# Where the Gelus of the third and fourth row groups stand against the last group's LayerNorm, in an attention and state-space kernel on one Trainium2 core

## The reference, cut to what matters

```python
yn = yg * rsqrt(mean(yg**2) + eps) * ssm_norm_w      # RMS norm of the gated scan
z1 = x1 + linear_ff(yn @ out_proj_w.T)               # first residual
h  = layernorm(z1, ln2_w, ln2_b)
out = z1 + linear_fc2(gelu(linear_fc1(h)))           # second residual, stored
```

## Time and profile before

| | kernel before |
|---|---|
| median of 3 runs | 310.67 us (310.57 to 311.52) |
| profiled execution, own time | 309.12 us |
| its span (first to last instruction) | 307.3 us |
| mean granted TensorE clock | 0.901 of full speed |
| PE busy | 239.4 us (78%) |
| DVE busy | 204.6 us (67%) |
| ACT busy | 166.6 us (54%) |
| POOL busy | 115.1 us (37%) |
| DMA | 12.96 MB, mean 42 GB/s |

### The profile page before, as it was taken

How to read it: one execution, slowest core, us unless ns; L and a number is a source line. 1 busy time by engine, 2 the same in 40 slices (tenths; PEclk the granted TensorE clock), 3 DMA queues, 4 the chain that set the end, 5 groups by cost and what they waited for, 6 DMA issues and landing times.

```text
span 307.3 us, 8733 instructions
## 1 busy us (share of the span) xinstructions
PE 239.4 (78%) x3666; PEld 148.7 (48%) x3666; DVE 204.6 (67%) x335; ACT 166.6 (54%) x289; POOL 115.1 (37%) x94
## 2 busy tenths in 40 slices
PE   8963878985979768658568799979999948956653
PEld 3642555663757445527564456524544424434421
DVE  2798667879398646353725968997867785484323
ACT  2255466766377683544248644673558328723291
POOL 1613194375234600004001975483968742300000
PEclk9998599999699999596977999997999979997768
DMA  6923021100111100043144000000000000011003
GB/s 179 327 31 105 34 70 45 63 36 36 36 36 55 54 2 5 1 101 69 33 99 101 0 2 2 2 3 0 5 2 0 2 0 2 2 34 36 1 0 68
DMA packets 25222, 12.96 MB, mean 42 GB/s; under 512 B 22240, under 2 KB 22496, under 8 KB 25056
## 3 DMA queue, kind: packets, MB, share of 16 engines
q1 hardware_dynamic: 23456, 11.24, 13.7%
q10 hardware_dynamic: 1728, 1.17, 1.5%
HBM read 4.63 MB, written 1.05 MB: 18 GB/s over the span
## 4 chain that ended last, share of the span: by engine, by line
PE 42%; DVE 30%; ACT 14%; issue 12%; DVEq 0%; ACTq 0%
PE ring L575 20%; PE score L575 8%; PE p_turn L575 6%; PE oz L575 4%; DVE s_cen L1134 4%; DVE rot_cos L1075 3%; PE ring L580 2%; DVE rot_sin L1079 2%; DVE mix L1224 2%; DVE ln_s L910 2%; DVE ln_v L930 2%; DVE xhat L945 2%; ACT prob_t L1375 2%; DVE cen L918 2%; ACT ln_l L936 1%
## 5 line engine op out<-in xcount | busy, mean ns | idle before, releaser
L1595 POOL TENSOR_TENSOR a_msk<-dt_fin,c_sb 128x512 f32<-128x512 f32 x32 | 40.0, 1249 | 33.6 <-DVE dt_fin L1051 23.8
L1224 DVE TENSOR_TENSOR mix<-dec,g_m 128x512 f32<-128x512 f32 x32 | 31.4, 987 | 2.2 <-ACT dec L1461 1.5
L1122 DVE TENSOR_REDUCE s_max<-score 128x16 f32<-128x1024 f32 x16 | 19.6, 1222 | 14.6 <-PE score L575 14.5
L1375 ACT ACTIVATE prob_t<-p_turn 128x512 f32<-128x512 f32 x32 | 17.6, 594 | 15.5 <-PE p_turn L580 15.0
L1580 POOL TENSOR_TENSOR dtx<-xv,dt_fin 64x512 f32<-64x512 f32 x16 | 19.8, 1238 | 13.2 <-PE p_turn L575 12.2
L925 ACT ACTIVATE sqr<-cen 128x512 f32<-128x512 f32 (+1 forms) x13 | 7.7, 595 | 31.0 <-DVE cen L918 31.0
L575 PEld LDWEIGHTS p_turn<-mix,dtx 128*32 128x32 f32 x512 | 11.0, 110 | 27.5 <-issue 14.7
L575 PE MATMUL score<-a_msk,c_sb 128*128 128x512 f32 x44 | 24.3, 635 | 0.0
L954 POOL TENSOR_TENSOR k_rot<-rot_cos,rot_swap 128x512 f32<-128x512 f32 x7 | 8.9, 1275 | 35.3 <-DMA rot_swap<-rot_sin 35.3
L1385 ACT ACTIVATE prob<-s_cen 128x1024 f32<-128x1024 f32 x16 | 16.8, 1053 | 9.5 <-DVE s_cen L1134 9.5
L575 PE MATMUL oz<-prob_t,v_bd 128*32 128x64 f32 x512 | 11.3, 234 | 12.4 <-ACT prob_t L1375 9.3
(11 more groups left out here) (185 smaller groups left out, 579.7 us busy)
## 6 DMA issues: line engine op xcount, KB each, us to landing
rot_swap<-rot_sin SPq DMA_DIRECT2D x28, 128.0 KB, 2.1
p_sb<-params SPq DMA_DIRECT2D x1, 1520.0 KB, 10.9
x_tok<-x SPq DMA_DIRECT2D x16, 64.0 KB, 4.0
ut_a<-u SPq DMA_DIRECT2D x8, 126.0 KB, 2.6
ut_b<-u SPq DMA_DIRECT2D x8, 124.0 KB, 2.5
ut_b<-u SPq DMA_DIRECT2D x8, 122.0 KB, 2.5
out<-x_tok SPq DMA_DIRECT2D x10, 64.0 KB, 2.2
back<-x ACTq DMA_DIRECT2D x4, 128.0 KB, 6.5
```

The source lines that it names most:

```text
L1122: v.tensor_reduce(s_max[:, n % 2, :], sc, AX, ALU.max).then_inc(s_maxed, 1)
L1224: v.tensor_tensor(mix[:, e % LAPS, :, :], dec[:, e % LAPS, :, :], wide(g_m[:, e // 4 % 2, e % 4, :], SSM_H), ALU.mult)\
L1375: a.activation(prob_t[:, e % 2, 4 * hp:4 * hp + 4, :].rearrange("p k n -> p (k n)"), PT[hp], ACT.Identity)\
L1595: gp.tensor_tensor(a_msk[:, m % LAPS, :, :], deep(dt_fin[:, 0, SSM_H * m:SSM_H * (m + 1)], GRID), wide(cst("tri"), SSM_H), ALU.mult).then_ ...
```

## The change

Two edits in the tables that order the tail:

```diff
@@ -103,7 +103,7 @@
-MLP_STEPS = ((28, 29, 30), (28, 30, 31), (36, 37, 38), (37, 38, 39), (38, 39, 40))
+MLP_STEPS = ((28, 29, 30), (28, 30, 31), (37, 38, 39), (38, 39, 40), (38, 39, 40))
@@ -126,9 +126,10 @@
         steps[PROJ_STEP[o] + 1].append(("yo", o))
     for o in range(len(GROUPS)):
+        steps[NORM_STEP[o]].append(("ht", o))
+    for o in range(len(GROUPS)):
         for kind, at in zip(("f1", "f2", "fo"), MLP_STEPS[o]):
             steps[at].append((kind, o))
-        steps[NORM_STEP[o]].append(("ht", o))
     return before, steps
```

## The result

The kernel after took 309.01 us (median of 20 runs, 306.95 to 313.55), the kernel before 309.06 us (median of 20 runs, 303.87 to 311.75): no difference that can be told. The runs spread over 8 us before and 7 us after, so these medians can't tell a change of 0.3% (0.93 us) from none. By it the kernel after is 0.8% slower, by the medians it is level; neither says that it is faster, and both lie within 2%.

What follows compares the result with a forecast made beforehand. ACT with its table loads was taken as the bound. Removed loads against f1(2)'s later place, PE's queue, clock and store queues summed to +0.3 us on 310.67, so 311.0 us, range 309.5 to 312.0.

Steps and rivals of the forecast that it cites:

- slower: the clock: Rival, chance 0.15: PE at 1.2 GHz between 294.2 and 301 costs 1.0, up to 1.8 us; 311.7 to 312.5.
- the sum: Net effect on the kernel's end: +0.3 us, ends -0.4 and +1.0, with TensorE's clock rising at 299.
- What goes: On ACT, three table loads (3.85 us) go, so the last group's xhat(4) runs at 293.2, 4.65 us sooner.
- What comes: On PE, f1(2) stands behind the turn of ht(4): f2(2) 2.6 us late, f_2(2) about 1.2 late.
- The queue on PE ahead of fo(2): On PE, fo(2) now waits for f1(3) and f1(4), 1.06 us each at 1.2 GHz, 1.12 together at 2.4.
- the low case: TensorE's clock low until f1(3) and f1(4) are done (301.0): fo(2) turns from 300.85, 1.0 us lost.
- The clock: TensorE's rise to 2.4 GHz, between 298 and 301, taken at 299; store queues then end 0.3 us later.
- clock up as before: TensorE at 2.4 GHz from 297.6: last addition 1.2 us sooner, store queues swallow two thirds, 0.4 us gained.
- The stores: Last two store pairs queue behind group 3's addition: 2 x 1.25 us on SPq, 1.4 a pair on ACTq.
- faster: Rival, chance 0.14: TensorE's clock stretches fall otherwise on the ladder, gaining 0.95 or 1.8 us; 308.9 to 309.7.
- the load behind its wait: Rival, chance 0.04: ACT's load for Gelu(2) waits for f1(2)'s product, costing up to 1.2 us; 312.0.
- the loads stay: Rival, chance 0.02: ACT's logarithm and exponential at 292.6 would carry two loads, 2.6 us; 313.5.

Runs made afterwards that it cites:

- e1: The change's first edit alone, on the kernel before, so f1(2) stays ahead of ht(4); median 307.86 us against 308.36 of before, ratio 1.0121.
- e10: The kernel after, unchanged, profiled a third time; single time 309.71 us.
- e9: The kernel after, unchanged, profiled once more; single time 310.24 us.
- e12: A second profiled execution of the same kernel as e6; single time 306.28 us.
- e4: Kernel before with last LayerNorm one step earlier, f1(2) and f1(3) ahead of ht(4), f1(4) between f2(2) and fo(2); median 306.41 us, ratio 1.0034.
- e6: Kernel after with products of no use filling PE's two pauses; median 307.77 us against 307.63 of before, ratio 0.9999.
- e3: Kernel after with the stores of groups 3 and 4 merged into one; median 308.95 us, ratio 1.0037 against before.
- e5: Kernel before with the stores of groups 3 and 4 merged into one; median 307.46 us, ratio 0.994 against before.
- e11: The kernel before, unchanged, profiled once more; single time 310.88 us.
- e7: The order of e4 and the merged store of e3 together; median 305.87 us against 307.63 of before, ratio 0.9937.
- e2: Kernel before with the set of logarithm and exponential requested once behind Gelu(2); median 306.42 us against 308.36 of before, ratio 1.0011.
- e8: Kernel after with f1(3) one step earlier, directly behind f1(2); median 307.02 us against 307.63 of before, ratio 0.992.

## Why the prediction was right

The forecast of no change fits: the medians of 20 runs differ by 0.05 us. That they agree so closely is luck, since the runs of one kernel spread over 7 to 8 us and can't confirm 0.3%. Both medians lie 1.6 us and more below the three runs that the prediction started from, so its 311.0 is high by 2.0, most of which is the base and not the change; taken as microseconds, its range of 309.5 to 312.0 begins 0.5 us above the measured 309.01, and only as a difference from before does the range hold. The loads, the place of f1(2), the queue on PE and the store queues came as worked out. The course of the clock didn't, and with it the tail of the profile after came out like the rival "slower: the clock" and not like the sum. Point by point:

- *What goes.* Three loads went, xhat(4) came at T0 + 1.0 (forecast 293.2, which is T0 + 1.0), its turn at T0 + 1.6. The 1.38 us of drain that the Trainium skill adds to a load (ScalarE: Activation LUTs, "What ACT_TABLE_LOAD costs") never showed: Gelu(2) after starts 0.02 us behind its load too.
- *What comes.* f1(2) behind the turn cost what was worked out: f2(2) at T0 + 5.1, forecast 5.2. e1 shows that this place alone holds up f2(2) by 1.9 us and, at the same clock, the end by 1.1.
- *The queue on PE ahead of fo(2).* f1(3) and f1(4) stood there, and fo(2) started at T0 + 8.6; the low case had 300.85, or T0 + 8.7.
- *The clock.* I took a rise at 299, T0 + 6.8. Measured were about T0 + 8.4 and, twice, 9.4. This step of the sum was mis-sized: the rise behind f1(4), costed at +1.0 to +1.8, is what happened in the first profile and in e10, and in e9 it came nearly as late. A clock at 1.2 GHz beyond 301 us, or T0 + 8.8, was named as a sign that the forecast is wrong, and two of the three profiles showed it. The reason given for a late rise, PE's pauses, is borne out in course A alone: e12 against e9 moves the rise by 3.5 us, e4 against e1 by almost 7. In course B the rise was at T0 + 5.6 with and without pauses. What the prediction couldn't see from one trace is that the course before T0 matters as much as the tail's own work.
- *The case "clock up as before".* It was costed with additions ending at 300.9, 302.4 and 302.8, or T0 + 8.7, 10.2 and 10.6, and 0.4 us gained. e6, the order of after with the clock up from T0 + 5.6, had 8.8, 10.2 and 10.7 and gained 0.3 at the end of the span. So the sum is right where its clock is.
- *The stores.* That the queues would run back to back and set the end was right. I counted the last two pairs behind the addition of group 3; on ACT's queue it was all three, 1.44 us each, behind the addition of group 2. In the first profile after, that gives T0 + 10.35 + 4.33 + 1.8 = 16.5 (measured 16.49); the sum's way, from the addition of group 3 with 2.8 us, gives 16.4. The prediction asked for SPq alone whether the store of group 2 is out before the next; on ACT's queue it ended at T0 + 11.9, 0.1 us behind the addition of group 3. The price of the queues is confirmed by e3 and e5.
- *Why it evens out all the same.* Against the profile that I had, the tail after is 0.8 to 1.4 us longer, where the sum said 0.3. The medians show nothing of it. What the rival "faster" said of before, that its ladder may fall into a stretch of 1.2 GHz, was seen in e11: 1.5 us longer, 16.6. Within a course the order of after is ahead by 0.3 (B, by e6) or 0.7 us (A); in course C its price or gain isn't known. How often each kernel meets each course in its runs isn't known either, since only profiled executions show the clock by stretches. So that the mix of these makes the medians equal is argued from five profiles, not shown.

The rival with the load behind its wait is out: in the timeline of ACT after, the load starts before the product has ended. So is the one in which the loads stay: there is one load in place of four.

## What to carry to other kernels

A function's table load taken off the path gains only as far as the next wait in line: ask at once what the moved operation's input was doing, and keep a product in the idle time that it had. The order of products on PE counts twice: by what stands ahead of a short turn, and by whether PE runs unbroken, since from the same clock before T0 the unbroken run of e4 and e7 brought 2.4 GHz back at T0 + 1.6 and the runs with pauses of e1 and e9 at T0 + 8.4. Before a difference of a microsecond between two profiles is put down to a change, look whether the clock ran alike up to the place where the change first acts. Additions that come together need their stores merged, those that come apart don't.

## What the runs showed of the hardware that wasn't expected

- The program up to T0 is nearly the same in all ten kernels, and yet T0 lay between 286.2 us (e5) and 295.6 us (e6). One profile's total can't judge a change of a microsecond; a count from a common event can, if the clock before it ran alike.
- A function without its set is not always one load: with the Gelu's set present, logarithm and exponential each brought their own; a request for the set with both took one (e2).
- Two DMAs of a pair take 1.25 us to issue on SP's queue and 1.3 to 1.53 on ACT's, whatever their size here: the merged pair of twice the size lengthened the time behind the last addition by only 0.28 us (e5).
- Filling PE's pauses with products that nobody reads raised the granted clock 3.5 us sooner and brought the end 1.3 us forward in one pair of executions (e12 against e9); with the clock of course B it rose at T0 + 5.6 filled or not (e6, e8).
- The clock came in three courses before T0, the same to a few tenths of a microsecond in each group of profiles, whichever kernel ran.
